# Seven products in place of eight for the query projection of a gated cross-attention block

## The reference

```
x = x + tanh(g_xattn) * attn(layernorm(x), ctx)
x = x + tanh(g_ffn)   * lora_experts(layernorm(x))

attn(latents, context):            # 32 query heads, 8 key/value heads, head size 128
    kv = concat(context, latents)  # 461 rows per batch element
    q = rms_norm(latents @ Wq) ; k = rms_norm(kv @ Wk) ; v = kv @ Wv
    out = softmax(q k^T / sqrt(128)) v      # four query heads share a key head
    return out @ Wo
lora_experts(x): top 2 of 8 experts of rank 16, gates normalised, times 0.5
```

## Time and profile before

| | |
|---|---|
| runs | 1750.63, 1753.11, 1757.34 us, median 1753.11 |
| profiled execution | 1748.85 us, span 1746.9 us |
| busy PE, DVE, ACT, POOL | 97%, 67%, 50%, 42% of the span |
| projection of keys and values | to 636.4 us |
| query blocks ahead of slot 0 | 636.4 to 684.5 us |
| slots 0 to 54 | 684.5 to 1309.0 us |
| last nine slots, output projection, experts | to the end |

### The profile page before, as it was taken

The page is one execution under the profiler, slowest core; times in us unless marked ns, Lnnn a source line. Parts: engine busy times, 40 slices in busy tenths (PEclk is TensorE's granted clock), DMA queues, the critical chain, the costliest instruction groups (busy, mean ns, idle before and its releaser), DMA issues.

```text
span 1746.9 us, 26303 instructions
## 1 busy us (share of the span) xinstructions
PE 1692.9 (97%) x9312; PEld 1508.2 (86%) x9312; DVE 1170.6 (67%) x2074; ACT 879.1 (50%) x1655; POOL 730.5 (42%) x584
## 2 busy tenths in 40 slices
PE   7999999999999999999999999999998999999996
PEld 6788888678888879999999999999997888999994
DVE  6778876777777733777777777777766664455546
ACT  5455554454544423666666666666656654343321
POOL 1444543234443402666666666666665550000000
PEclk9999999999999999999999999999999999999999
DMA  5567778545566554344444333444444654665522
GB/s 193 163 185 237 231 213 247 140 145 173 158 176 161 138 214 144 120 122 123 131 130 123 119 122 120 131 131 130 127 126 160 207 181 160 218 218 191 194 102 66
DMA packets 215654, 278.13 MB, mean 159 GB/s; under 512 B 51956, under 2 KB 187956, under 8 KB 210020
## 3 DMA queue, kind: packets, MB, share of 16 engines
q1 hardware_dynamic: 214948, 269.90, 49.7%
q10 hardware_dynamic: 576, 6.55, 0.9%
HBM read 189.77 MB, written 86.64 MB: 158 GB/s over the span
## 4 chain that ended last, share of the span: by engine, by line
PE 87%; DVE 5%; ACT 3%; issue 2%; DMA 2%; POOL 0%; SPq 0%; DVEq 0%; ACTq 0%; POOLq 0%
PE bank L757 26%; PE bank L759 25%; PE bank L758 25%; PE bank L895 5%; PE bank L862 2%; PE bank L791 1%; DVE mx L1652 1%; PE bank L1045 1%; DMA at_raw<-at_d 1%; DMA kT<-kT_d 1%; DVE wo_lo L1672 1%; ACT w_hi L1111 1%; DVE pT_lo L1646 1%; DMA wr<-Wkv 0%; ACT pT_hi L1286 0%
## 5 line engine op out<-in xcount | busy, mean ns | idle before, releaser
L739 POOL TENSOR_SCALAR pr<-pr,rr 100x461 f32<-100x461 f32 x256 | 382.8, 1501 | 299.0 <-DVE rr L1667 299.0
L757 PE MATMUL bank<-w_hi,a_hi 128*128 128x512 f32 (+1 forms) x856 | 340.7, 398 | 12.2 <-DVE a_lo L1442 9.3
L759 PE MATMUL bank<-w_hi,a_lo 128*128 128x512 f32 (+1 forms) x856 | 334.9, 391 | 0.0
L758 PE MATMUL bank<-w_lo,a_hi 128*128 128x512 f32 (+1 forms) x856 | 334.3, 391 | 0.0
L1295 ACT ACTIVATE pr<-bank,nm,rq 100x461 f32<-100x461 f32 x256 | 188.6, 737 | 170.9 <-DVE nm L1658 167.8
L1652 DVE TENSOR_REDUCE mx<-bank 100x1 f32<-100x461 f32 x256 | 161.7, 632 | 81.4 <-PE bank L759 76.1
L757 PEld LDWEIGHTS bank<-w_hi,a_hi 128*128 128x128 f32 (+1 forms) x856 | 157.8, 184 | 49.5 <-issue 10.4
L759 PEld LDWEIGHTS bank<-w_hi,a_lo 128*128 128x128 f32 (+1 forms) x856 | 157.5, 184 | 38.0
L757 PE MATMUL bank<-xT_hi,wq_hi 128*128 128x400 f32 x512 | 188.2, 368 | 0.5 <-issue 0.5
L757 PE MATMUL bank<-at_hi,wo_hi 128*128 128x400 f32 x512 | 183.1, 358 | 5.7 <-DVE at_lo L1683 2.9
L758 PEld LDWEIGHTS bank<-w_lo,a_hi 128*128 128x128 f32 (+1 forms) x856 | 158.0, 185 | 34.8
(11 more groups left out here) (133 smaller groups left out, 3496.1 us busy)
## 6 DMA issues: line engine op xcount, KB each, us to landing
wo_raw<-Wo SPq DMA_DIRECT2D x32, 1024.0 KB, 4.9
kT_d<-kst SPq DMA_DIRECT2D x56, 512.0 KB, 5.2
v_d<-vst SPq DMA_DIRECT2D x56, 512.0 KB
at_raw<-at_d SPq DMA_DIRECT2D x32, 800.0 KB, 7.2
kT<-kT_d SPq DMA_DIRECT2D x64, 361.0 KB, 4.7
kvr<-ctxT SPq DMA_DIRECT2D x44, 512.0 KB, 5.8
wq_raw<-Wq SPq DMA_DIRECT2D x32, 512.0 KB, 6.0
vv<-v_d SPq DMA_DIRECT2D x64, 240.0 KB
```

Source lines behind the costliest of these rows:

```text
L739: pool.tensor_scalar(pr[0:NQ, u % 2, i], pr[0:NQ, u % 2, i], rr[0:NQ, i:i + 1], None, ALU.mult).then_inc(p_done, 1)
L757: pe.matmul(o, lh, rh, start=start, stop=False, skip_group_check=more)
L758: pe.matmul(o, lh, rl, start=False, stop=False, skip_group_check=more)
L759: return pe.matmul(o, ll, rh, start=False, stop=stop, skip_group_check=more)
```

## The change

The query projection becomes 16 steps (`QSTEPS`) that continue the list: a step takes two heads, both halves of the batch elements and both halves of the 1024 inputs, in seven products of four parts each, 1,344 matmuls of the same shape. Now the latents' sums are one side and the sums of `Wq` blocks the other.

- The latents' seven operands are made in steps 18 to 25 from latents stored unsplit (`xq_d`): POOL four sums, ACT seven copies, DVE seven subtractions for each of four pairs of batch elements. They go to DRAM (`store_pair`) and come back as `xw` (two operands, early) and `xv` (five, issued by ACT in the last projection step).
- `Wq` of a pair of heads is loaded into `kvr` and goes through the projection's own sums, splits and ring. From step `QK0` = 32 on there is one buffer for it (`slot_of`).
- 16 products (`LEAD`) are made ahead of slot 0, then seven parts per slot, four slots a step. `query_bank` alternates two PSUM banks.
- Blocks come out by copies (`keep_query`, ACT, three a step) and by sums and a copy (`query_result`, DVE, four a step). `copy_queries` and `wq_split` go.
- The memory map is new. The output projection's weights share memory with latents' operands, so chunks 0 and 1 are loaded in iteration u = 53.

The core of the diff (helpers of the list, of waits and of the map are cut):

```diff
+QORDER = (P1, P2, P6, P5, P7, P3, P4)
+SEQ += [(_k, _o) for _k in range(STEPS, ALL) for _o in QORDER]
+LEAD = 16
...
+X_ORDER = (0, 1, 5, 2, 4, 6, 3)
+XS = NT + 3
...
+def slot_of(k):
+    return k % 2 if k < STEPS + 2 else 0
...
+            def load_pair(n):
+                if n == 0:
+                    sp.wait_ge(w_plain, 8)
+                    sp.wait_ge(w_lo_done, 8)
+                else:
+                    sp.wait_ge(xls_done, 7 * n)
+                sp.dma_start(xp[:, 0], xq_d[:, TB + n]).then_inc(xp_in, 16)
+                sp.dma_start(xp[:, 1], xq_d[:, n]).then_inc(xp_in, 16)
+            def store_pair(n):
+                sp.wait_ge(xls_done, 7 * n + 7)
+                for src, dst in ((xhs, xh_d), (xls, xl_d)):
+                    sp.dma_start(dst[:, :, n]..., src[:]...).then_inc(xs_stored, 16)
...
             for u in range(UNITS):
-                load_heads(u + AHEAD)
                 if u == OUT0 - 2:
+                    sp.wait_ge(prod_done, POS[ALL - 1, P6] + 1)
+                    load_chunk_weights(0)
+                    load_chunk_weights(1)
                     load_chunk(0)
                     load_chunk(1)
...
+                if 1 <= u and u + 1 < UNITS:
+                    load_kT(u + 1)
+                load_heads(u)          # u % 4 < 2: load_kv(QK0 + u // 4 + 1, u % 4)
...
 POOL, slots:
+                k = QK0 + u // 4
+                if u % 4 == 0 and QK0 < k < ALL:
+                    last_sum(k)
+                if u % 4 == 2 and k + 1 < ALL:
+                    sums(k + 1)
+                if u % 4 == 3 and k + 1 < ALL:
+                    second_sum(k + 1)
                 if u + 1 < UNITS:
                     unit_rms(u + 1)
...
 PE:
+                mm = three(ps[query_bank(k, o)][:, 0:TW]..., a_hi[:, s, c], a_lo[:, s, c],
+                           hi[:, :, c], lo[:, :, c], start and c == 0, c == KC - 1, not start)
...
+                if u % 4 == 3:
+                    squares(n + 2)
                 c_(0)
...
+                if u == 0:
+                    squares(n - 1)
+                else:
+                    if u % 4:
+                        squares(n + (0, 1, 3)[u % 4 - 1])
                 c_(2)
...
                 c_(6)
-                c_(7)
...
 ACT, within the last projection step:
+            def load_x(i, n, m):
+                act.wait_ge(xs_stored, 32 * TB)
+                act.dma_start(xv_hi[:, n - 2:m - 2]..., xh_d[:, n:m]).then_inc(xop_in[i], 16)
+                act.dma_start(xv_lo[:, n - 2:m - 2]..., xl_d[:, n:m]).then_inc(xop_in[i], 16)
+   after P2: load_x(1, 2, 4); after P6: load_x(2, 4, 5); after P5: load_x(3, 5, 7)
...
 DVE, slots (turn = u % 4):
                 maxima(u, 0)
                 if prev:
                     p_split(u - 1, 0)
-                if n < 2 * H:
-                    copy_queries(n)
+                if turn == 0:
+                    query_result(n)
+                if turn == 1:
+                    operand_of(k, P3)
+                if turn == 2:
+                    query_result(n + 1)
+                if turn == 3:
+                    if (n + 2) % QB == QB - 2:
+                        mean_squares(n + 2)
+                    query_result(n + 3)
                 maxima(u, 1)
                 inverse(u, 0)
                 if prev:
                     p_split(u - 1, 1)
                 inverse(u, 1)
+                if turn == 0:
+                    operand_of(k, P5)
+                if turn == 1:
+                    operand_of(k, P4)
+                if turn == 2:
+                    operand_of(k + 1, P1)
+                if turn == 3:
+                    operand_of(k + 1, P2)
                 maxima(u, 2)
...
                 inverse(u, 3)
+                if turn == 0:
+                    operand_of(k, P7)
+                if turn == 2:
+                    query_result(n + 2)
                 if u + 1 < UNITS:
                     q_split(u + 1)
-                if n < 2 * H:
-                    next_wq(n)
+                if turn == 3:
+                    operand_of(k + 1, P6)
```

More of the change, by code:

```diff
@@ L138, in cols, with rows_of, step_before, block_of @@
     return min(P, ROWS_M - t * P)
+def rows_of(k):
+    return cols(k % NT) if k < STEPS else P
+def slot_of(k):
+    return k % 2 if k < STEPS + 2 else 0
+def step_before(k):
+    return max(n for n in range(k) if slot_of(n) == slot_of(k))
+def block_of(n):
+    r = n % 4
+    return n // 4 * 2 + r % 2, (1, 0, 0, 1)[r]
 def build(nc, x, ctxT, Wq, Wkv, Wo, AR, BmT, vecs, rows, out):
@@ L379, in kv_need @@
         def kv_need(k):
-            return 16 * sum(1 + (n % NT == MIXED) for n in range(k % 2, k + 1, 2))
+            return 16 * sum(1 + (n < STEPS and n % NT == MIXED) for n in range(k + 1) if slot_of(n) == slot_of(k))
         def a_src(i):
             k, o = OPS[i]
-            raw = kvr[:, k % 2]
-            n = cols(k % NT)
+            raw = kvr[:, slot_of(k)]
+            n = rows_of(k)
             if k in PLAIN:
@@ L722, in at_product @@
                     last_sum(k)
-                if o == P5 and k + 1 < STEPS and k + 1 not in PLAIN:
+                if o == P5 and k + 1 not in PLAIN:
                     sums(k + 1)
+                if (k, o) == (STEPS - 1, P4):
+                    second_sum(STEPS)
+                if (k, o) in XSUM_AT:
+                    latents_sum(*XSUM_AT[k, o])
                 if o == P2 and 0 <= k - 1 - X0 < B:
                     latent_rstd(k - 1 - X0)
-            for j in range(PRODUCTS + 3):
+            for j in range(PRE):
                 at_product(j)
@@ L861, in squares @@
                     o = ps[SS][0:NQ, c0:c0 + 2]
[L862 removed]
+                    mm = pe.matmul(o, sq[n % 2][:, bb * NQ:(bb + 1) * NQ], ones[:], start=True, stop=True)
                 mm.then_inc(ss_done, 1)
[L865 to L871 removed]
+            for j in range(PROJ):
+                at_product(j)
+            for j in range(PROJ, PRE):
+                k, o = SEQ[j]
+                n = 4 * (k - STEPS)
+                if ("turn0", j) in WHEN:
+                    turn_keys(WHEN["turn0", j], 0)
+                if ("turn1", j) in WHEN:
+                    turn_keys(WHEN["turn1", j], 1)
+                if o == P7:
+                    squares(n)
+                if o in (P1, P2, P6) and k > STEPS:
+                    squares(n - 3 + QORDER.index(o))
+                for c in range(KC):
+                    query_part(k, o, c)
             def scores(u, i):
```

588 lines of the change are left out of this document (350 added, 238 removed).

## The result

The changed kernel takes 1780.24 us, median of four runs (1777.64 to 1783.16), beside 1752.71 for the kernel before (four runs, 1750.63 to 1757.34): a ratio of 1.0154, 95% interval 1.0128 to 1.018. That is 1.5% slower, clear of the noise, where 1738 us and a gain were forecast, and outside the range of 1721 to 1768.

The account below looks back on a forecast made before the run. PE's matmuls were taken to bound the kernel, with 1.4 us of slack in a cross-engine loop. Slots -20.6, lead -5.2, projection +3, keys +7.5 gave -15.3 us: 1753.1 to 1738 us, range 1721 to 1768 (forecast's own 1730 to 1746).

Parts of the forecast that it names:

- Matmuls and the saving itself: Whole kernel: 1,536 matmuls become 1,344, 192 x 0.185 = 35.5 us less on PE if nothing else binds.
- DVE's free time: Steady slots: 4.7 us of DVE work out, 7.2 in, leaving 9.6 of 43.3 us free over four slots.
- rival 1: Slots: PE's whole saving comes, turn 0's loop stays below PE and bursts are covered; -30, 1723 us; chance 0.12.
- The other turns stay PE's: Steady slots: turns 1, 2 and 3 bound by PE at 10.83, 10.83 and 11.48 us; 44.0 for four slots.
- `a_lo` inside the loop: Each slot, after inverse 1: it takes 0.69 us, the third nm regains 0.43; loop 10.24 us, under PE's 10.83.
- Rival 2: Slots: DVE and POOL exclude each other for a whole scale; 46.0 us for four slots, 1764 us; chance 0.23.
- The last scale of turn 0: Turn 0, after inverse 3: P7's `a_lo` makes POOL's scale slip by 0.45 us; turn 0 takes 10.9, not 10.18.
- Second half of the projection: Before the query products: DMA share rises to 0.93, key stores queue behind pairs' stores; 3 us lost (0 to 12).
- Rival 4: Projection's second half: store bursts cost their upper end, 12 us; 1747 us; chance 0.08.
- Ahead of slot 0: First query matmul to slot 0: 42.9 us, 5.2 less (3 to 7), with 1 us for late operands.
- Keys of u = 54: Before unit 54's scores: chunk weights queue ahead of its keys; wait about 9 us, 7.5 us more (5 to 9).
- rival 3: Slots, turn 2: `Wq` weights in their single buffer land late for POOL's sums; 1759 us; chance 0.12.

Follow-up runs that it names:

- first profile: Profiled execution of the changed kernel without further edits, beside the kernel before; span 1781.3 us, median of its runs 1780.24 us.
- the run of stores one by one: Changed kernel with a pair's fourteen operand stores sent one operand at a time, 0.2 MB each, instead of two of 1.4 MB; 1767.2 us, 1.0080 of before.
- after: The changed kernel itself, without further edits, against the kernel before: 1780.24 us, ratio 1.0154.
- the run with late keys: Changed kernel with the last projection step's key turns, splits and stores moved to later query products; 1768.2 us, 1.0100 of the kernel before.
- second profile: The changed kernel run again with no edit, on the follow-up runs' chip: 1776.5 us, 1.0140 of the kernel before.
- the last run: Changed kernel plus later keys and P7 low half, single-operand stores, unit-54 keys first, POOL waiting for q_lo, squares and third-block result earlier; 1730.6 us, 0.9871 of before.

## Why the prediction was wrong

**Matmuls and the saving itself: right.** 192 matmuls fewer, a part still 0.555 us. Once the waits are taken away the slots take 600.9 us for 624.5, 23.6 less, where 20.6 less was forecast for them, and the lead 43.5, where 42.9 was. That the sums agree so closely is in part luck: four slots took 43.85 for 44.0, with turn 0 at 10.32, not 10.9, since this run no longer makes P7's low half ahead of the last scale, and with turn 2 at 11.12, not 10.83. Two slips in the working change nothing: DVE's free time comes to 8.7 us by its rows, not 9.6, and rival 1 to 1722 us, not 1723.

**"The other turns stay PE's": wrong, the step that failed in the slots.** I followed one loop, from turned probabilities to the scales, and not the edge that closes the slot: scores of u+1 wait for q_lo(u+1), which DVE makes during POOL's last scale. I put four sums into POOL's queue directly behind that scale and counted only whether POOL had time. Turns 1 and 2 were to take 10.83 us each and took 11.84 and 11.52. 0.68 of the first is turn 0's late scale, the rest of both is mostly q_lo, and 0.16 for the squares in turn 2. Worth: 44.0 forecast, 45.2 measured, 17 us over 55 slots, the largest of the misses; the edits for scale and q_lo brought 43.85. In all the forecast missed the span by 49.8 us: 22.3 in slots 0 to 54, 13.9 ahead of the first query matmul, 11.5 from there to slot 0, 2.1 behind.

**`a_lo` inside the loop: right.** 0.67 to 0.68 us after inverse 1 in each slot, the third nm 0.16 for 0.59. Rival 2 as I priced it, a delay of this `a_lo` up to the scale's end, did not occur. By the Trainium skill, "SBUF — State Buffer", section "Who interferes with whom", the port pair that DVE and GpSimd share is an exclusive lock, and a DVE instruction with two SBUF inputs contends with a GpSimd instruction that reads SBUF. The `a_lo` of 0.67 us inside a scale disagrees. The q_lo of 4.16 us, which ends after a scale and two sums, agrees that DVE is shut out. What decides between the two is open.

**The last scale of turn 0: right mechanism, mis-sized.** A slip of 0.45 us was forecast; the scale lengthened by 0.85 (2.29 for 1.44), since q_lo followed the `a_lo` at once and I had counted only the `a_lo`. The cost falls into turn 1, not turn 0 (10.24 for 10.9).

**Second half of the projection: mis-sized.** I named the queue (key stores behind the pairs' stores) and put 3 us on it, 0 to 12. It cost 15.2 us in the first profile, 9.4 of it waits for `kn` and 5.1 the lower clock after them, and 11.6 to 13.0 in the seven other profiles with the same stores. I set the 5 us that operands are made ahead against a burst; what ran out was the single `kst`: PE waits for normalised keys, these for the key split on ACT and DVE, ACT for a store of 10 to 13.7 us. The clock was in no term. The DMA share, put at 0.93, was 0.77, which agrees with the run of stores one by one that it was not the total of bytes. Rival 4 had the right place, and its 12 us is what those seven profiles show within 1 us.

**Ahead of slot 0: wrong.** I asked whether the 8.2 MB would be there for P3, the sixth product, and they were: the last landed at 664.3, 25 us after the first was issued, and no product of after waited for them. I did not ask who stands behind them: the last key store (23.0 us) and the weights of the next step (24.5 us in the run with late keys, where they are what PE feels). That is the forecast -5.2 against +6.3 (+4.4 in the second profile): 9.8 us of waiting, and 2.5 us for the 17 matmuls at the lower clock level behind it.

**Keys of u = 54: right.** A wait of about 9 us was forecast, 6.50 measured; 7.5 us were forecast as loss, 5.4 measured in the slot itself and 6.2 with the next one. When the keys go first, these two slots are 8.5 us shorter than in after, more than was lost, for the kernel before had a wait there too.

**Late weights in the slots (rival 3): did not occur.** Landings had a median of 4.5 us. POOL waited for weights once, in the lead.

Open: why a sum that is ready but not next holds DVE off, how POOL and DVE hand over, and what is left of the begin, 642.2 for 636.4. Of these 5.8 us 1.3 are there within the first 30 us; 4.5 are lost in the second half, where PE still waits 3.7 us in five places, three of them on `kn`. The longest of those, 1.5 us at 609, is the one behind the `xw` loads, and no run moved these. Turn 2 also keeps 0.29 us over its 10.83 in the last run, of which I can name only the 0.16 for the squares that the trace of after shows.

## What to carry to other kernels

A large transfer is priced by what is asked for behind it, from any queue, and by who works in order behind that: ask for each small store and load issued in the next microseconds (here some 10 behind a pair's stores, 25 behind the operands) who waits for its buffer. A wait of PE is priced above its length where the clock falls with it: six waits of after, of 2.1 to 9.8 us, have a stretch at the lower level beside them. Work put on an idle engine is priced at its neighbours: list what the other engines do in its first and last microsecond, and follow every wait that the first instruction of a stage has, not only the last one to come in. An order that is free for one engine can be worth as much as the arithmetic saved; here a handful of orders, one wait and smaller stores turned +1.4% into -1.3%.

## What the hardware showed that I had not expected

- A DVE subtraction of 400 columns that starts 0.17 us into a POOL scale of 1.44 takes 0.90 us if POOL has nothing else ready, mostly 1.6 if a sum with two SBUF inputs is ready next or next but one, and once 4.16. One semaphore wait in front of the sum is enough to bring back 0.90. Two DVE instructions back to back, the first begun 0.18 us before a scale, do the same to POOL: 2.29 us for 1.44.
- The place in the scale matters: `a_lo` starting 0.77 us into a scale ran undisturbed in every steady slot (0.67 to 0.68 us).
- In the run with late keys the DMA engines moved 400 GB/s at a share of 0.99 for 24 us, above the 336 from which I had worked out the operands. In after, operand loads issued first in that stretch took 7 to 12 us, the store of 0.5 MB issued 4 us behind them 23.
